# One TensorE kernel of two mixes and two grouped convolutions: the 32-column tiles of both convolutions put side by side

## The chip, the cores and the metric

The kernel runs on one core of one Trainium2 chip. The metric is the device time in microseconds of one execution; the time before is the median of three runs. The engines run beside each other and are kept in step by semaphores: TensorE (PE in the profile, its weight loads PEld), VectorE (DVE), ScalarE (ACT), GpSimd (POOL), and the queue of SyncE (SP) that issues the DMAs.

## The reference, cut to what matters

For each of 128 samples, x is 128 channels by 2048 points. Four layers are added to x one after the other; layers 0 and 2 are a mix of the channels with a matrix of the sample's own, layers 1 and 3 a grouped convolution with 9 taps.

```python
# layers 0 and 2
att = softmax(gelu(gelu(e @ W0 + b0) @ W1 + b1) @ W2 + b2)
agg_w = einsum('bk,koi->boi', att, weight[..., 0])
x = x + einsum('boi,bih->boh', agg_w, x) + (att @ bias_k)[:, :, None]
# layers 1 and 3
out = conv(x, weight, stride 1, padding 4, feature_group_count=4)   # 9 taps
x = x + out + einsum('nd,od->no', c, c_weight)[:, :, None] + side[None, :, None]
```

## The kernel before, in words

A sample's 2048 points are cut into 4 phases (point modulo 4) of 512 points, so a bank of PSUM (512 float32 a lane) holds one phase or one group. There are 4 groups of 32 channels, which are the four quarters of the lanes. The adding of x is an identity inside the weights.

A convolution is done for all 4 phases at once: of the 12 shifts (`SHIFTS`) between an input phase and an output phase, the 6 in the middle (`DENSE`) have weights for all four output phases and the 3 at either end only for one, two or three.

- `dense` (L348 to L364) does the 6 middle shifts. Each operand is split into a high and a low float32r part and three products are made (`PASSES`), for each of 4 groups: 6 x 3 x 4 = 72 matmuls with tiles of 32 rows by 128 columns. Four of them, one for each group, stand in the array side by side, so there are 18 rounds.
- `sparse` (L330 to L346) does the outer shifts with plain float32 operands. `NARROW` is one lot of tiles of 32 by 32, four output phases for each of four groups, 16 matmuls. `WIDE` is two lots of tiles of 32 by 64, two tiles for each of four groups, 8 matmuls each. The trace has two weight loads and two matmul records for each float32 matmul, so `NARROW` is 32 records of loads and each lot of `WIDE` 16.

A text here speaks of D for a stretch with 32x128 tiles, N for the 32x32 lot and W for the 32x64 lots, with the number of the layer: N1, W1, D1 for the first convolution (banks 4 to 7), N3, W3, D3 for the second (banks 0 to 3).

All engines run one program of steps `i` = 0 to 128, and the samples are pipelined over them. TensorE in step `i` (L390 to L413) does layer 1 of sample `i`, layer 3 of sample `i - 1`, layer 2 of sample `i` (`second_mix`, 48 matmuls of 32x128) and layer 0 of sample `i + 2` (`first_mix`, 12 matmuls of 128x128). Before the change its order is D1, N1, W1, W3, N3, D3, second mix, first mix. A matmul lot that ends a bank raises `mm[l]`.

What the other engines do in step `i`, in this order:

- ScalarE (L572 to L583): `full_0(i+1)` (bank to `y1_full`, frees banks 0 to 3), `high_2(i-1)`, `x_high(i+2)`, `high_1(i)` (waits for `mm[1]`, which the last lot of layer 1's `sparse` raises), `high_0(i+1)`, `output(i-1)` (waits for `mm[3]`, the end of D3), `full_2(i)` (waits for the second mix).
- VectorE: `matrix(0)` and `halves(0)` of sample i+2 (the last of it waits for the first mix before), `low_2(i-1)`, `x_low(i+2)`, `low_1(i)` (waits for `high_1`), `matrix(2)` and `halves(2)` of sample i+1, `low_0(i+1)`.
- GpSimd: small bias copies, and `in_time(i-2)` (L787), which waits until the shuffle DMAs have landed.
- SP (L226 to L239), strictly in order: the load of x, the store of the output, `store_matrix(i+1)` (waits for `own_set[2]`, the end of `halves(2)`), 16 shuffle DMAs of sample i-1, 4 loads of the mixing matrix (`load_matrix`, L207), which the next second mix needs.

D1 waits for `low_set[0]` (the end of `low_0`) and bank by bank for `full_2`; N3 or W3 reads `y3_full` and writes banks 0 to 3; D3 waits for `low_set[2]`; the second mix for `low_set[1]` and for its matrix.

Of the kernel before, what the change touches and what calls it, by code (L numbers as in the profile page):

```python
# [5 lines left out]
def build_cond_resid(nc, x, small, mix_w, mix_b, conv_w, consts, scratch, out):  # L6
# [10 lines left out]
    N = T // PH  # L17
# [7 lines left out]
    WIDE = (((1, 0, 2), (10, 2, 2)), ((2, 0, 2), (9, 2, 2)))  # L25
    NARROW = (((0, 0, 1), (9, 1, 1), (2, 2, 1), (11, 3, 1)),)
# [5 lines left out]
    with ctx:  # L32
        def sb(name, shape, dt=fp32):
            return ctx.enter_context(nc.sbuf_tensor(name, shape, dt))

        def sem(name):
            return ctx.enter_context(nc.semaphore(name))
# [4 lines left out]
        y1 = sb("y1", [128, 2, PH, HALO], f32r)  # L42
        y1_full = [sb(f"y1_full{b}", [128, PH, HALO]) for b in range(2)]
        y2 = sb("y2", [128, 2, G, N], f32r)
        y3 = sb("y3", [128, 2, PH, HALO], f32r)
        y3_full = sb("y3_full", [128, PH, HALO])
# [72 lines left out]
        conv_ident_set, conv_set = sem("conv_ident_set"), sem("conv_set")  # L119
# [18 lines left out]
        full_set = [sem(f"full_set{l}") for l in range(3)]  # L138
        high_set = [sem(f"high_set{l}") for l in range(3)]
        low_set = [sem(f"low_set{l}") for l in range(3)]  # L140
        phases_set = sem("phases_set")
# [16 lines left out]
        def has(i, inner, lag):  # L158

            return inner or 0 <= i - lag < B  # L160

        def nth(j, k):

            return 4 * j + k + 1
# [90 lines left out]
        def _(pe):  # L255
# [27 lines left out]
            for l in range(2):  # L283
                pe.wait_ge(att_set, l + 1)
                nc.tensor.matmul(ps[:, 2 + l, 0:K], ident[:, 0:1].broadcast_to([128, 128]), att_sb[:, l, :],
                                 start=True, stop=True).then_inc(att_first_mm, 1)
# [8 lines left out]
            def side_bias():  # L295

                pe.wait_ge(ctx_in, 16)
                pe.wait_ge(full_set[0], 2)
                for l in range(2):
                    for g in range(G):  # L300
                        last = nc.tensor.matmul(ps[:, l, g * B:(g + 1) * B], ctx_w_sb[:, l, g, :], emb_sb, start=True, stop=True)  # L301
                    last.then_inc(ctx_mm, 1)
# [24 lines left out]
                            if final:  # L327
                                ins.then_inc(mm[2], 1)

            def sparse(layer, src, begins, wait_bank):  # L330

                bank = 4 if layer == 1 else 0
                lots = WIDE + NARROW if begins else NARROW + WIDE
                for r, units in enumerate(lots):
                    for t in range(G):
                        rows = slice(CG * t, CG * (t + 1))
                        if r == 0 and begins:
                            wait_bank(t)
                        for s, p, width in units:
                            q, p_in = divmod(s, PH)  # L340
                            final = r == len(lots) - 1 and not begins
                            ins = nc.tensor.matmul(ps[CG * p:CG * (p + width), bank + t, :],  # L342
                                                   conv_raw[layer][rows, 128 * s + CG * p:128 * s + CG * (p + width)],
                                                   src[rows, p_in, q:q + N], start=(r == 0 and begins), stop=final)
                            if final:
                                ins.then_inc(mm[1], 1)  # L346

            def dense(layer, src, begins, wait_bank):  # L348

                bank = 4 if layer == 1 else 0  # L350
                order = sorted(DENSE, key=lambda s: (s % PH, s))
                for k, s in enumerate(order):
                    q, p_in = divmod(s, PH)
                    for n, (w, a) in enumerate(PASSES):
                        first = k == 0 and n == 0 and begins
                        final = k == len(order) - 1 and n == len(PASSES) - 1 and not begins
                        for t in range(G):
                            rows = slice(CG * t, CG * (t + 1))
                            if first:
                                wait_bank(t)  # L360
                            ins = nc.tensor.matmul(ps[:, bank + t, :], conv_parts[layer][rows, w, s - DENSE[0], :],  # L361
                                                   src[rows, a, p_in, q:q + N], start=first, stop=final)
                            if final:
                                ins.then_inc(mm[3], 1)  # L364

            def step(i, inner, odd):

                def free1(t):
                    if not inner and i == B - 1:
                        pe.wait_ge(full_set[2], 4 * i)  # L370
                    elif inner or i > 0:
                        pe.wait_ge(full_set[2], nth(i - 1, t))
                    elif t % 2 == 0:
                        pe.wait_ge(table_act, 2 - t // 2)
                    else:
                        pe.wait_ge(table_dve, 2 - t // 2)

                def free3(t):
                    if has(i, inner, -1):
                        pe.wait_ge(full_set[0], nth(i + 1, t))  # L380
                    else:
                        pe.wait_ge(phases_set, nth(i - 2, t))

                def free0(q):
                    if inner or i > 0:
                        pe.wait_ge(phases_set, nth(i - 1, q))
                    else:
                        pe.wait_ge(full_set[0], nth(1, q))

                if has(i, inner, 0):  # L390
                    if not inner and i == 0:
                        pe.wait_ge(zeros_set, 1)
                        pe.wait_ge(conv_set, 1)
                    pe.wait_ge(low_set[0], 4 * (i + 1))
                    dense(1, y1, True, free1)
                    if not inner and i == 0:
                        side_bias()
                        pe.wait_ge(full_set[0], G)
                    sparse(1, y1_full[odd], False, free1)
                if not inner and i == 0:  # L400
                    pe.wait_ge(ctx_read, 2)
                    first_mix(1, lambda q: pe.wait_ge(full_set[0], nth(0, q)))
                if has(i, inner, 1):
                    if not inner and i == 1:
                        pe.wait_ge(conv_set, 2)
                    pe.wait_ge(full_set[2], 4 * i)
                    sparse(3, y3_full, True, free3)
                    pe.wait_ge(low_set[2], 4 * i)
                    dense(3, y3, False, free3)
                if has(i, inner, 0):  # L410
                    second_mix(i)
                if has(i, inner, -2):
                    first_mix(i + 2, free0)  # L413
# [13 lines left out]
            for q in range(G):  # L427
                nc.tensor.matmul(ps[:, q, :], m_sum[0][:], x_t[:, q, :], start=True, stop=True).then_inc(mm[0], 1)  # L428
            att_to_all(1)
            all_steps(pe, step)  # L430
            last_regroup()

# [455 lines left out]
```

## Time and profile before

| | |
|---|---|
| median of 3 runs | 2650.08 us (2649.07 to 2650.8) |
| profiled execution, its own time | 2650.44 us |
| its span in the trace | 2648.6 us |
| PE busy | 2627.4 us (99%) |
| DVE busy | 2143.3 us (81%) |
| ACT busy | 2034.7 us (77%) |
| POOL busy | 818.0 us (31%) |
| L342 (`sparse`) matmuls | 16384 records, 753.8 us busy |
| L361 (`dense`) matmuls | 18432 records, 1141.7 us busy |

"Busy" is the time in which at least one instruction of the engine was under way. A matmul's end is modelled in the trace, so the start of the next weight load or matmul says more than a busy share. The difference between the profiled execution's own time and its span, 1.8 us, lies before the first and after the last instruction.

### The profile page before, as it was taken

The page shows a single profiled execution, that of the slowest core. Times are in us where ns is not written, and L with a number is a line of the kernel's source. Part 1 is how long each engine was busy: PE and PEld are TensorE (multiplying, and loading weights), DVE is VectorE, ACT ScalarE, POOL GpSimd, SP SyncE. Part 2 cuts the span into 40 slices and gives each one's busy share as a digit, 9 for nine tenths or more (in the row PEclk, how much of TensorE's full clock was granted, in tenths as well). Part 3 has the DMA queues.
Part 4 walks back from the last instruction along what each step waited for, and adds up shares of the span by engine and source line. Part 5 has one row for each costly group of instructions (what it writes and reads, how often), then busy time and mean ns, then how long its engine had stood idle before and what let it go on. Part 6 is the DMA issues. An engine that isn't in the chain of part 4 may idle for free.

```text
span 2648.6 us, 106673 instructions
## 1 busy us (share of the span) xinstructions
PE 2627.4 (99%) x42610; PEld 1808.4 (68%) x42610; DVE 2143.3 (81%) x3093; ACT 2034.7 (77%) x3605; POOL 818.0 (31%) x1040
## 2 busy tenths in 40 slices
PE   9999999999999999999999999999999999999997
PEld 6667666766676667666766676667666766676665
DVE  8888788878887888788878887888788878887884
ACT  7777777777777777777777777777777777777774
POOL 1233233323332333233323332333233323332332
PEclk9999999999999999999999999999999999999999
DMA  4565556555655565556555655565556555655554
GB/s 166 182 205 185 180 184 195 187 180 184 196 187 180 184 195 187 180 183 196 187 180 183 194 189 180 183 195 188 180 183 195 188 180 183 195 189 180 182 176 149
DMA packets 228046, 489.82 MB, mean 185 GB/s; under 512 B 47016, under 2 KB 129072, under 8 KB 195376
## 3 DMA queue, kind: packets, MB, share of 16 engines
q1 hardware_dynamic: 228016, 489.39, 58.7%
q8 instruction: 22, 0.36, 0.1%
q14 instruction: 8, 0.07, 0.0%
HBM read 205.04 MB, written 150.99 MB: 134 GB/s over the span
## 4 chain that ended last, share of the span: by engine, by line
PE 98%; DVE 1%; ACT 0%; issue 0%; DVEq 0%; ACTq 0%
PE ps L361 42%; PE ps L342 28%; PE ps L313 14%; PE ps L326 13%; DVE y L680 0%; DVE y L674 0%; DVE xp L652 0%; DVE m_sum L632 0%; DVE prod L627 0%; PE ps L259 0%; DVE y_full L703 0%; PE ps L428 0%; PE ps L301 0%; PE ps L264 0%; DVE x_t L715 0%
## 5 line engine op out<-in xcount | busy, mean ns | idle before, releaser
L361 PE MATMUL ps<-y,conv_parts 32*128 32x512 f32 x18432 | 1141.7, 395 | 3.9 <-DVE y_full L703 1.8
L361 PEld LDWEIGHTS ps<-y,conv_parts 32*128 32x128 f32 x18432 | 906.5, 183 | 283.1 <-issue 131.4
L781 POOL COPY bias<-bias_table 128x4 f32 (+3 forms) x512 | 317.6, 621 | 1795.5 <-DMA o_ch<-o_ph 896.9
L680 DVE TENSOR_TENSOR y<-y_full,y 128x512 fp32r<-128x512 f32 x1020 | 636.6, 688 | 221.9 <-ACT y L497 221.9
L342 PE MATMUL ps<-y_full,conv_raw 32*32 32x512 f32 (+1 forms) x16384 | 753.8, 596 | 1.7 <-DVE y_full L703 1.7
L491 ACT ACTIVATE y_full<-ps,bias 128x512 f32<-128x512 f32 x1016 | 602.6, 707 | 26.6 <-issue 16.2
L546 ACT ACTIVATE o_ph<-ps,bias 128x512 f32<-128x512 f32 x508 | 308.5, 693 | 371.5 <-PE ps L361 371.5
L497 ACT CAST y<-y_full 128x512 fp32r<-128x512 f32 x1020 | 566.8, 663 | 0.7 <-DVE y_full L703 0.7
L342 PEld LDWEIGHTS ps<-y_full,conv_raw 32*32 32x32 f32 (+1 forms) x16384 | 275.5, 116 | 408.4 <-issue 406.2
L787 POOL COPY o_t<-o_ch 128x512 f32<-128x512 f32 x508 | 528.5, 1186 | 26.9 <-DMA o_ch<-o_ph 26.9
L491 ACT ACTIVATE y<-ps,bias 128x512 fp32r<-128x512 f32 x516 | 313.0, 690 | 191.3 <-PE ps L342 176.6
L674 DVE SCALAR_TENSOR_TENSOR y<-ps,bias,y 128x512 fp32r<-128x512 f32 x516 | 352.0, 746 | 117.1 <-ACT y L491 117.0
L313 PE MATMUL ps<-xp,m_own 128*128 128x512 f32 x1524 | 386.9, 402 | 0.8 <-DVE xp L652 0.8
L326 PE MATMUL ps<-y,m_parts 32*128 32x512 f32 x6144 | 384.3, 391 | 0.8 <-DVE y L674 0.8
L627 DVE TENSOR_TENSOR prod<-mix_sb,att_table 128x1152 f32<-128x1152 f32 x254 | 379.3, 1493 | 0.0
L632 DVE TENSOR_REDUCE m_sum<-prod 128x128 f32<-128x1152 f32 x256 | 346.4, 1353 | 8.8
L326 PEld LDWEIGHTS ps<-y,m_parts 32*128 32x128 f32 x6144 | 335.8, 183 | 23.4 <-issue 1.6
L313 PEld LDWEIGHTS ps<-xp,m_own 128*128 128x128 f32 x1524 | 275.9, 187 | 105.5 <-issue 47.4
L652 DVE TENSOR_TENSOR xp<-x_t,xp 128x512 fp32r<-128x512 f32 x508 | 316.5, 686 | 0.0
L467 ACT CAST xp<-x_t 128x512 fp32r<-128x512 f32 x508 | 283.2, 671 | 0.6 <-DMA x_t<-x 0.6
L642 DVE CAST m_own<-m_sum 128x128 fp32r<-128x128 f32 x255 | 65.6, 257 | 119.7 <-PE ps L313 103.4
L645 DVE TENSOR_TENSOR m_own<-m_sum,m_own 128x128 fp32r<-128x128 f32 x255 | 74.6, 292 | 8.8
(60 smaller groups left out, 74.6 us busy)
## 6 DMA issues: line engine op xcount, KB each, us to landing
x_t<-x SPq DMA_DIRECT2D x128, 1024.0 KB, 5.0
o_ch<-o_ph SPq DMA_DIRECT2D x2032, 64.0 KB, 2.0
out<-o_t SPq DMA_DIRECT2D x127, 1024.0 KB, 4.0
m_parts<-mixed SPq DMA_DIRECT2D x512, 128.0 KB, 2.6
mixed<-m_own SPq DMA_DIRECT2D x128, 128.0 KB, 1.7
conv_raw<-conv_w SPq DMA_DIRECT2D x2, 768.0 KB, 9.8
mix_sb<-mix_w SPq DMA_DIRECT2D x2, 576.0 KB, 7.4
out<-x_t SPq DMA_DIRECT2D x4, 256.0 KB, 4.2
```

The costliest lines, as they stand in the source:

```text
L313: ins = nc.tensor.matmul(ps[:, q, :], m_own[0][:, m, :], xp[:, a, q, :], start=(n == 0), stop=(n == len(PASSES) - 1))
L326: ins = nc.tensor.matmul(ps[:, 4 + p, :], m_parts[rows, g, m, :], y2[rows, a, g, :], start=first, stop=final)
L342: ins = nc.tensor.matmul(ps[CG * p:CG * (p + width), bank + t, :], conv_raw[layer][rows, 128 * s + CG * p:128 * s + CG * (p + width)], src ...
L361: ins = nc.tensor.matmul(ps[:, bank + t, :], conv_parts[layer][rows, w, s - DENSE[0], :], src[rows, a, p_in, q:q + N], start=first, stop=f ...
L491: nc.scalar.activation(dst, src, ACT.Identity, bias=bias[layer][:, k % WIDTH[layer]:k % WIDTH[layer] + 1]).then_inc(done[layer], 1)
L497: nc.scalar.copy(dst, full).then_inc(high_set[layer], 1)
L627: nc.vector.tensor_tensor(prod[layer][:], mix_sb[layer][:], att.broadcast_to([128, C, K + 1]), ALU.mult).then_inc(scaled[layer], 1)
L632: nc.vector.tensor_reduce(m_sum[layer][:], prod[layer][:], AX_X, ALU.add).then_inc(summed[layer], 1)
L674: nc.vector.scalar_tensor_tensor(out=dst, in0=src, scalar=bias[layer][:, k % WIDTH[layer]:k % WIDTH[layer] + 1], in1=high.bitcast(fp32), o ...
L680: nc.vector.tensor_tensor(dst, full, high.bitcast(fp32), ALU.subtract).then_inc(low_set[layer], 1)
L781: nc.gpsimd.tensor_copy(bias[layer][:], bias_table[:, bass.ds(j, 1), COLUMN[layer]:COLUMN[layer] + WIDTH[layer]].rearrange("c j g -> c (j ...
L787: nc.gpsimd.tensor_copy(ov[:, p, :], o_ch[:, p, :]).then_inc(in_time_set, 1)
```

## The change

TensorE's order in a step becomes D1, N1, N3, W1, W3, D3, second mix, first mix: `sparse` is called with one list of lots at a time, N1 then N3, W1, W3. For i = 0 (no layer 3) and i = 128 (no layer 1) the missing ones are left out. The accumulation flags follow: N3 begins banks 0 to 3, the last lot of W1 ends banks 4 to 7 and raises `mm[1]`. The waits of layer 3 (`y3_full` whole, banks 0 to 3 free, and in step 1 the second convolution's low parts) move into `third_ready`, which `dense` calls for D1 before the last of its six shifts. Nothing is changed on other engines, and no matmul is added or taken away.

```diff
-            def sparse(layer, src, begins, wait_bank):
+            def sparse(layer, src, lots):
                 bank = 4 if layer == 1 else 0
-                lots = WIDE + NARROW if begins else NARROW + WIDE
                 for r, units in enumerate(lots):
...
-                            final = r == len(lots) - 1 and not begins
+                            final = layer == 1 and units is WIDE[-1]
...
-                                                   src[rows, p_in, q:q + N], start=(r == 0 and begins), stop=final)
+                                                   src[rows, p_in, q:q + N], start=(layer == 3 and units is NARROW[0]), stop=final)
...
+                    if k == len(order) - 1:
+                        wait_last()
...
-                def free3(t):
-                    if has(i, inner, -1):
-                        pe.wait_ge(full_set[0], nth(i + 1, t))
-                    else:
-                        pe.wait_ge(phases_set, nth(i - 2, t))
+                def third_ready():
+                    if not inner and i == 1:
+                        pe.wait_ge(conv_set, 2)
+                    if has(i, inner, 1):
+                        pe.wait_ge(full_set[2], 4 * i)
+                    if has(i, inner, 1) and has(i, inner, -1):
+                        pe.wait_ge(full_set[0], 4 * (i + 2))
+                    elif has(i, inner, 1):
+                        pe.wait_ge(phases_set, 4 * (i - 1))
...
-                    dense(1, y1, True, free1)
+                    dense(1, y1, free1, third_ready)
...
-                    sparse(1, y1_full[odd], False, free1)
+                    sparse(1, y1_full[odd], NARROW)
+                else:
+                    third_ready()
+                if has(i, inner, 1):
+                    sparse(3, y3_full, NARROW)
+                if has(i, inner, 0):
+                    sparse(1, y1_full[odd], WIDE)
...
-                    pe.wait_ge(full_set[2], 4 * i)
-                    sparse(3, y3_full, True, free3)
+                    sparse(3, y3_full, WIDE)
                     pe.wait_ge(low_set[2], 4 * i)
-                    dense(3, y3, False, free3)
+                    dense(3, y3, lambda t: None, lambda: None)
```

## Rows read from the trace of the kernel before

**Rows 1.** The page's chain that ended last, shares of the span by engine

```profile
PE 98%; DVE 1%; ACT 0%; issue 0%; DVEq 0%; ACTq 0%
```

**Rows 2.** Timeline, weight loads, one step: start us, length us, what, [idle before]

```profile
1000.29 4.04 PEld L361 LDWEIGHTS ps<-y,conv_parts 32*128 32x128 f32 x72 [0.36 <-issue]
1004.69 0.23 PEld L342 LDWEIGHTS ps<-y_full,conv_raw 32*32 32x32 f32 x32 [0.35 <-issue]
1005.76 0.29 PEld L342 LDWEIGHTS ps<-y_full,conv_raw 32*64 32x64 f32 x16 [0.84 <-issue]
1006.24 0.23 PEld L342 LDWEIGHTS ps<-y_full,conv_raw 32*64 32x64 f32 x8 [0.19 <-issue]
...
1008.39 0.23 PEld L342 LDWEIGHTS ps<-y_full,conv_raw 32*64 32x64 f32 x8 [0.20 <-issue]
1009.43 0.23 PEld L342 LDWEIGHTS ps<-y_full,conv_raw 32*32 32x32 f32 x32 [0.81 <-issue]
1010.51 4.02 PEld L361 LDWEIGHTS ps<-y,conv_parts 32*128 32x128 f32 x72 [0.84 <-issue]
...
1017.70 2.62 PEld L313 LDWEIGHTS ps<-xp,m_own 128*128 128x128 f32 x12 [0.37 <-issue]
1020.67 4.04 PEld L361 LDWEIGHTS ps<-y,conv_parts 32*128 32x128 f32 x72 [0.36 <-ACT y_full L491]
```

**Rows 3.** Timeline, ScalarE, the same step

```profile
1007.77 2.42 ACT L491 ACTIVATE y<-ps,bias 128x512 fp32r<-128x512 f32 x4 [1.47 <-PE ps L342]
...
1015.21 2.43 ACT L546 ACTIVATE o_ph<-ps,bias 128x512 f32<-128x512 f32 x4 [2.92 <-PE ps L361]
1017.86 4.74 ACT L491 ACTIVATE y_full<-ps,bias 128x512 f32<-128x512 f32 x8 [0.22 <-issue]
```

**Rows 4.** Timeline, VectorE, the same step and the head of the next

```profile
1008.49 2.73 DVE L674 SCALAR_TENSOR_TENSOR y<-ps,bias,y 128x512 fp32r<-128x512 f32 x4 [0.88 <-ACT y L491]
...
1014.53 0.29 DVE L645 TENSOR_TENSOR m_own<-m_sum,m_own 128x128 fp32r<-128x128 f32 x1
1014.74 2.49 DVE L680 TENSOR_TENSOR y<-y_full,y 128x512 fp32r<-128x512 f32 x4
...
1020.78 0.23 DVE L642 CAST m_own<-m_sum 128x128 fp32r<-128x128 f32 x1 [0.90 <-PE ps L313]
...
1023.13 2.50 DVE L680 TENSOR_TENSOR y<-y_full,y 128x512 fp32r<-128x512 f32 x4 [1.80 <-ACT y L497]
```

**Rows 5.** Timeline, SP's issues, the same step and the next

```profile
1015.92 10.04 SPq L214 DMA_DIRECT2D o_ch<-o_ph  x16
1026.15 1.88 SPq L207 DMA_DIRECT2D m_parts<-mixed  x4
```

**Rows 6.** Timeline, weight loads behind the last wait

```profile
2637.56 0.24 PEld L421 LDWEIGHTS ps<-y_full,consts_sb 32*32 32x32 f32 x32 [2.06 <-DVE y_full L710]
```

**Rows 7.** Timeline, weight loads of step 1

```profile
41.80 4.04 PEld L361 LDWEIGHTS ps<-y,conv_parts 32*128 32x128 f32 x72 [1.53 <-DVE y L680]
...
56.68 2.67 PEld L326 LDWEIGHTS ps<-y,m_parts 32*128 32x128 f32 x48 [0.66 <-issue]
```

**Rows 8.** Timeline, VectorE, step 1

```profile
44.91 0.95 DVE L602 TENSOR_TENSOR conv_parts<-conv_raw,conv_parts 128x768 fp32r<-128x768 f32 x1
...
53.84 2.72 DVE L674 SCALAR_TENSOR_TENSOR y<-ps,bias,y 128x512 fp32r<-128x512 f32 x4
```

**Rows 9.** Timeline, SP's issues, an early step (the fourth)

```profile
100.47 11.66 SPq L214 DMA_DIRECT2D o_ch<-o_ph  x16
112.40 3.21 SPq L207 DMA_DIRECT2D m_parts<-mixed  x4
```

**Rows 10.** Timeline, GpSimd, the same early steps

```profile
95.22 3.99 POOL L787 COPY o_t<-o_ch 128x512 f32<-128x512 f32 x4
...
115.60 3.98 POOL L787 COPY o_t<-o_ch 128x512 f32<-128x512 f32 x4
```

**Rows 11.** Timeline, VectorE, the same early step

```profile
96.75 2.58 DVE L642 CAST m_own<-m_sum 128x128 fp32r<-128x128 f32 x1
```

More of the change, by code:

```diff
@@ L336, in sparse, with dense @@
                         rows = slice(CG * t, CG * (t + 1))
-                        if r == 0 and begins:
-                            wait_bank(t)
                         for s, p, width in units:
                             q, p_in = divmod(s, PH)
-                            final = r == len(lots) - 1 and not begins
+                            final = layer == 1 and units is WIDE[-1]
                             ins = nc.tensor.matmul(ps[CG * p:CG * (p + width), bank + t, :],
                                                    conv_raw[layer][rows, 128 * s + CG * p:128 * s + CG * (p + width)],
-                                                   src[rows, p_in, q:q + N], start=(r == 0 and begins), stop=final)
+                                                   src[rows, p_in, q:q + N], start=(layer == 3 and units is NARROW[0]), stop=final)
                             if final:
                                 ins.then_inc(mm[1], 1)
-            def dense(layer, src, begins, wait_bank):
+            def dense(layer, src, wait_bank, wait_last):
+                begins = layer == 1
                 bank = 4 if layer == 1 else 0
@@ L403, in step @@
                 if has(i, inner, 1):
-                    if not inner and i == 1:
-                        pe.wait_ge(conv_set, 2)
-                    pe.wait_ge(full_set[2], 4 * i)
-                    sparse(3, y3_full, True, free3)
+                    sparse(3, y3_full, WIDE)
                     pe.wait_ge(low_set[2], 4 * i)
-                    dense(3, y3, False, free3)
+                    dense(3, y3, lambda t: None, lambda: None)
                 if has(i, inner, 0):
```

## The prediction, made before the changed kernel was run

> **What bounds the kernel now.** I read the chain that ended last first. It is TensorE for 98% of the span [rows 1], so a cut on any other engine is worth nothing, and a cut in TensorE's own time is worth its whole size as long as nothing else comes late. Next I read the timeline of the weight loads over one step, because a matmul's end is only modelled and a load's start is recorded [rows 2]. A step is 20.38 us (1000.29 to 1020.67). D1 runs to 1004.69, N1 to 1005.76, W1 with W3 to 1009.43, N3 to 1010.51, then D3, the second mix, the first mix from 1017.70. The reader is to look at the rhythm of the loads in the W stretch: after the first burst of 16, bursts of 8 start at 1006.24 and so on to 1008.39, six bursts, five intervals, 0.43 us each. Four lots of W follow each other there (two of layer 1, two of layer 3), each with two passes, and the step from layer 1 to layer 3, where the kernel has five waits, keeps the same rhythm. Each burst starts and ends inside the pass ahead of it. So, inside one tile shape, a pass costs 0.43 us and its loads nothing.
>
> Where the shape changes the rhythm breaks. N1 is two passes and should take 0.86 us; it takes 1.07 (1004.69 to 1005.76), and N3 1.08. The W stretch is eight passes, 3.44 us, and takes 3.67. Each visit to a shape thus pays 0.21 to 0.23 us beyond its passes: its first loads in the open and the emptying at the end.
>
> **The change part by part.**
>
> *Fewer visits.* Before, a step visits N, W, N between D1 and D3: 5.82 us. After, it visits N, W: N1 with N3 is four passes plus one visit's surcharge, 4 x 0.43 + 0.21 = 1.93 us, and W stays at 3.67, together 5.60. The cut is one surcharge, 0.21 (from N1), 0.22 (N3) or 0.23 (W); I take 0.215. The trace does not show two N lots in a row, nor W followed by D. For the first the nearest row is W to W, at no cost; for the second, N3 to D3 and N1 to W1 end after the same time (1.08 and 1.07) though the shape behind them differs, so I take leaving to cost the same whatever comes next. The bounds are 0.23 us a step as gain, and on the other side a gain of nothing, if the loads of N3 lay open as the first burst of a visit does (0.23 us for 32 of them). Below nothing lies only a shortage of instructions: the pair of N lots asks for 128 records in 1.93 us where the W rhythm asks for 16 in 0.43. If TensorE were fed no faster than the W rhythm, 37 records a microsecond, the second 64 would take 1.73 us in place of 0.86, a loss of up to 0.87 less 0.215 = 0.65 us a step. Against it stands the last regroup: after a wait of 2 us the 32 loads of 16 tiles of 32x32 start within 0.14 us (0.24 less one load of 0.10) [rows 6]. I take no shortage.
>
> *Number of steps.* Both convolutions meet in steps 1 to 127. Step 1 I count apart, the other 126 give 126 x 0.215 = 27.1 us. Steps 0 and 128 have the same visits before and after.
>
> *The waits of layer 3, earlier.* They come in D1 before the last sixth, about 3.4 us after D1's start (5/6 of 4.04). `full_0` is last there: it ends at 1017.86 + 4.74 = 1022.60, which is 1.93 us after D1's start [rows 3]. `full_2` ends before that. Slack 1.4 us. Queued behind the wait are the last 12 matmuls of D1 and N1, none of which would start otherwise either before 3.4 us. A wait that is already met costs nothing visible at the W1 to W3 seam [rows 2]; bounds zero to 0.05 us a step (the five at that seam stay inside a rhythm read to 0.01), taken at zero.
>
> *Layer 1's end, later.* `mm[1]` is now raised behind N3: two passes later, 0.86 us. In the old step `high_1` starts at 1007.77 and becomes 1008.6. It had waited 1.47 us, and ScalarE waits 2.92 us before `output` [rows 3]; of this 2.92 the delay and the earlier end of D3 (0.215) take 1.07 and leave 1.8. So `output`, `full_2` and `full_0` keep their places behind D3. On VectorE `low_1` ends at 1008.49 + 2.73 = 1011.22 and becomes 1012.1; the second mix begins when D3's loads end, 1014.53, now 1014.3: slack 2.2. `low_0` ends at 1017.23 and becomes 1018.1; the next D1 starts at 1020.67, now 1020.45: slack 2.4. `halves(0)` waited 0.90 us for the first mix [rows 4]; this wait goes (0.90 - 0.86 - 0.215), and VectorE is 0.2 us late there, which the 1.80 us ahead of `low_2` absorbs. What is late next is therefore still TensorE's own stream.
>
> *SP and GpSimd.* `halves(2)` ends at 1014.82 [rows 4], now 1015.7. The store behind it is ahead of the 16 shuffles in SP's order, so the shuffles start at most 0.86 us later (1.1 us lay between 1014.82 and their old start at 1015.92, part of it to spare). They last 10.04 us and the four matrix loads behind them end their issue at 1028.03, 6.9 us ahead of the second mix at 1034.9 (1014.53 + 20.38) [rows 2, 5]. With 0.86 us later there and a need 0.43 us earlier (two steps' cuts), 5.6 us are left, for loads that land a few us behind their issue. Hidden.
>
> *Step 1.* The second convolution's low parts end at 44.91 + 0.95 = 45.86 [rows 8]. They used to be needed at N3's side, now they are waited for before the last sixth of D1, at 41.80 + 3.4 = 45.2 [rows 7]. TensorE stands 0.7 us; against 0.215 saved this makes D3 end 0.5 us later. The second mix there waited for `low_1` (53.84 + 2.72 = 56.56, start 56.68), 0.26 us of it with TensorE empty. Loss 0.3 us.
>
> *Sum.* 27.1 - 0.3 = 26.8 us. From the profiled execution's 2650.44 us this gives 2623.6; that execution lies 0.36 above the median of the runs, so I forecast 2623.3.
>
> *A page's rule against it.* The W rows show loads starting in full overlap with matmuls of the same four row groups [rows 2]. The Trainium skill, "TensorE: Matmul & The Clock Gate", Part 3, section "The mechanism", says that a weight load overlaps matmuls under way only when its row group is another one. By that rule N3's loads would wait for N1 in each row group, and its 0.23 us of loads would eat the saving: a sum of 2650. The trace's W rows disagree with it.
>
> **The rivals.**
>
> *The second N lot pays for its loads after all* (the mechanism of that sentence, kept for 16 tiles at once). For it: no row shows 16 tiles reloaded while they run; N has twice W's loads per pass. Against: W's burst of 8 takes 0.23 of 0.43 us and N's 32 take the same 0.23, so 16 have room. Price: 0.23 back of 0.215, no change, 2650; if half of them lie open 0.1 back, 2636.
>
> *The ring of SP and GpSimd becomes the bound.* In an early step shuffles, matrix loads, landing and `in_time` form a ring: `in_time` starts at 95.22 and at 115.60, 20.38 us apart, with the shuffles at 11.66 us instead of 10.04 and the matrix loads issued until 115.61 [rows 9, 10], and VectorE's cast takes 2.58 us beside `in_time`, where an undisturbed one takes 0.23 [rows 4, 11]. `in_time`'s end frees the output store, the cast's end the matrix store, and both are ahead of the shuffles on SP. If that ring stays at 20.38 or more while TensorE would like 20.16, it never recovers, the matrix comes late, and the gain is lost; with VectorE's 0.2 us of lateness inside it the step would be up to 20.38 + 0.2. That is 2650 to 2675 (126 x 0.2 = 25); its middle, 2663, stands for this rival. It decides from a ring of 20.38 us on. Against: in the old steady step the shuffles wait for `output` and not for the ring, with a cast of 0.23 us, and `in_time` has fallen back by itself.
>
> *Starved instructions*: up to 0.65 us a step as worked out, 2730 at the most; by [rows 6] unlikely.
>
> *A smaller surcharge saved*: if two joined N lots still cost 0.05 us at the seam, the gain is 126 x 0.165 = 21, 2629.
>
> **How the numbers follow.** Forecast as worked out, 2618 to 2627: 0.76. Smaller surcharge or half-open loads, 2627 to 2640: 0.14. Loads fully open, near 2650: 0.04. Ring: 0.04. Starved: 0.02. The range is 2617 to 2632; its lower end is 0.26 us saved a step, a bit over the W surcharge, its upper end 0.14. About 0.2%, 5.3 us, is what a measurement here can tell from no change. Faster by more: 0.90; within: 0.05; slower: 0.05.
>
> **What would show it.** Right: step length 20.16 us; 64 loads of 32x32 with one break of rhythm, N1 with N3 lasting 1.93 us; W at 3.67; `high_1`'s wait longer, `output`'s wait about 1.8 us, `halves(0)`'s wait gone. Wrong: a gap of 0.2 us between the two N bursts; matmuls of N3 spread out; weight loads of D1 or the second mix with a releaser on VectorE, ScalarE or DMA; casts of over 1 us in the middle of the run.

## The result and the profile after

The changed kernel takes 2659.22 us (median of 7 runs, 2658.56 to 2660.43) against 2650.8 us for the kernel before in 7 runs of the same sessions. The ratio is 1.0032, with a 95% interval of 1.0023 to 1.0042: slower by 8.4 us, beyond what the runs scatter. The forecast was 2623.3 with a range of 2617 to 2632. The sign was wrong, and the measured time lies 27 us above the range.

The page after shows the same picture as a whole. First its span and engine line, then its chain by engine, which answers to [rows 1]:

```profile
span 2656.6 us, 106246 instructions
PE 2635.7 (99%) x42610; PEld 1777.5 (67%) x42610; DVE 2103.8 (79%) x3093; ACT 2034.0 (77%) x3605; POOL 751.5 (28%) x1040
...
PE 98%; DVE 1%; issue 0%; ACT 0%; DVEq 0%; ACTq 0%
```

TensorE is still 98% of the chain, and its granted clock was 0.998 to 0.999 here and in every other run of this document, so the time has to be looked for inside its own stream. The timeline of the weight loads over one step, the view of [rows 2]:

```profile
1003.22 4.04 PEld L361 LDWEIGHTS ps<-y,conv_parts 32*128 32x128 f32 x72 [0.36 <-issue]
1007.62 0.23 PEld L339 LDWEIGHTS ps<-y_full,conv_raw 32*32 32x32 f32 x32 [0.35 <-issue]
1008.07 0.10 PEld L339 LDWEIGHTS ps<-y_full,conv_raw 32*32 32x32 f32 x1 [0.22 <-issue]
1008.50 0.55 PEld L339 LDWEIGHTS ps<-y_full,conv_raw 32*32 32x32 f32 x31 [0.32 <-issue]
1009.89 0.23 PEld L339 LDWEIGHTS ps<-y_full,conv_raw 32*64 32x64 f32 x16 [0.84 <-issue]
1010.38 0.18 PEld L339 LDWEIGHTS ps<-y_full,conv_raw 32*64 32x64 f32 x8 [0.25 <-issue]
...
1013.51 4.02 PEld L361 LDWEIGHTS ps<-y,conv_parts 32*128 32x128 f32 x72 [0.81 <-issue]
...
1020.70 2.62 PEld L313 LDWEIGHTS ps<-xp,m_own 128*128 128x128 f32 x12 [0.37 <-issue]
1023.68 4.04 PEld L361 LDWEIGHTS ps<-y,conv_parts 32*128 32x128 f32 x72 [0.36 <-ACT y_full L498]
```

A table of the two steps, each length the difference of two starts in these rows and in [rows 2]:

| stretch | before, us | after, us |
|---|---|---|
| D1 | 4.40 | 4.40 |
| N1 and N3 | 1.07 + 1.08 | 2.27 |
| W1 and W3 | 3.67 | 3.62 |
| D3 and second mix | 7.19 | 7.19 |
| first mix | 2.97 | 2.98 |
| step | 20.38 | 20.46 |

Steps of 20.46 and 20.43 alternate in the changed kernel, 0.065 us a step more than before on the mean, and 126 x 0.065 = 8.2 us is nearly the whole difference (8.4 measured, 8.0 between the spans). The change lies in two rows; the alternation lies in D3 and the second mix (7.19 and 7.17). W is 0.05 shorter. The pair of N lots, forecast at 1.93, takes 2.27, and that is more than the two lots took apart.

The third and fourth rows show how. N1's 32 loads come at once at 1007.62. At 1008.07, when N1's second pass starts, exactly one load of N3 is there; the next is at 1008.50, when that tile's first pass starts, and it is the same tile's second load. Then nothing. The instructions of that line in the gap from 1008.52 to 1008.69 and in the 0.4 us around it:

```profile
L339 PEld LDWEIGHTS ps<-y_full,conv_raw x1: 105/105/105, 1008.5 to 1008.5; 32*32 32x32 f32 x1
...
L339 PEld LDWEIGHTS ps<-y_full,conv_raw x13: 101/102/105, 1008.5 to 1008.8; 32*32 32x32 f32 x13
```

From the records of the single instructions (their starts in ns): N1's first second-pass matmul starts at 1008072 and a pass takes 427 to 429 ns, so it has streamed through at about 1008500. (This is what "complete" means below, the start of the last pass plus one pass. The end that the trace models for this matmul, 1008072 + 587 = 1008659, lies 0.16 us later.) The second tile of N3 loads at 1008690, and the 14 tiles behind it follow 16 to 17 ns apart, the last at 1008923. In N1, the tiles came 6 to 7 ns apart. So 15 of 16 tiles of N3 come late: 0.19 us after the first matmul of N1 is complete, and then at the pace of 17 ns a matmul. That is 0.19 + 14 x 0.0167 less the 0.10 that the lot's own spread takes anyway = 0.32 us, nearly the whole difference of 0.34 between 2.27 and 1.93.

The other engines' rows moved the way that was forecast. ScalarE and VectorE, answering to [rows 3] and [rows 4]:

```profile
1011.90 2.42 ACT L498 ACTIVATE y<-ps,bias 128x512 fp32r<-128x512 f32 x4 [2.69 <-PE ps L339]
...
1018.22 2.43 ACT L553 ACTIVATE o_ph<-ps,bias 128x512 f32<-128x512 f32 x4 [1.80 <-PE ps L361]
1020.86 4.74 ACT L498 ACTIVATE y_full<-ps,bias 128x512 f32<-128x512 f32 x8 [0.22 <-issue]
```

```profile
1018.60 2.49 DVE L687 TENSOR_TENSOR y<-y_full,y 128x512 fp32r<-128x512 f32 x4
...
1023.88 0.23 DVE L649 CAST m_own<-m_sum 128x128 fp32r<-128x128 f32 x1
...
1026.14 2.50 DVE L687 TENSOR_TENSOR y<-y_full,y 128x512 fp32r<-128x512 f32 x4 [1.71 <-ACT y L504]
```

`output` waits 1.80 us for D3, as forecast; `halves(0)` waits no longer; `low_0` ends at 1021.09, 2.6 us ahead of the next D1. None of them holds TensorE. The 1.80 is a hit by two errors that cancel: `high_1` starts 8.68 us behind D1's start and not 7.48, which is 1.20 later where 0.86 was forecast, and D3 starts 0.07 later where 0.215 earlier was forecast.

### The profile page after: what moved, and what is told of

Same layout as the page of the kernel before. It is cut to its first block, busy times and chain, and to the rows that moved or that the text cites. A ratio compares the mean times of both kernels' runs of the same rounds, so it can differ in the third digit from the quotient of the medians.

```text
span 2656.6 us, 106246 instructions
## 1 busy us (share of the span) xinstructions
PE 2635.7 (99%) x42610; PEld 1777.5 (67%) x42610; DVE 2103.8 (79%) x3093; ACT 2034.0 (77%) x3605; POOL 751.5 (28%) x1040
## 4 chain that ended last, share of the span: by engine, by line
PE 98%; DVE 1%; issue 0%; ACT 0%; DVEq 0%; ACTq 0%
PE ps L361 42%; PE ps L339 28%; PE ps L313 14%; PE ps L326 13%; DVE y L681 0%; DVE y L687 0%; DVE m_sum L639 0%; PE ps L259 0%; DVE prod L634 0%; DVE y_full L710 0%; ACT y L504 0%; DVE xp L659 0%; ACT y L498 0%; PE ps L435 0%; PE ps L301 0%
## 5 line engine op out<-in xcount | busy, mean ns | idle before, releaser
L339 PE MATMUL ps<-y_full,conv_raw 32*64 32x512 f32 (+1 forms) x16384 | 764.0, 596 | 1.6 <-DVE y_full L710 1.6
L788 POOL COPY bias<-bias_table 128x4 f32 (+3 forms) x512 | 235.5, 460 | 1869.3 <-DMA o_ch<-o_ph 944.3
L339 PEld LDWEIGHTS ps<-y_full,conv_raw 32*64 32x64 f32 (+1 forms) x16384 | 269.5, 117 | 428.0 <-issue 415.3
L794 POOL COPY o_t<-o_ch 128x512 f32<-128x512 f32 x508 | 522.5, 1156 | 27.0 <-DMA o_ch<-o_ph 27.0
L326 PEld LDWEIGHTS ps<-y,m_parts 32*128 32x128 f32 x6144 | 318.5, 183 | 40.1 <-issue 1.0
L634 DVE TENSOR_TENSOR prod<-mix_sb,att_table 128x1152 f32<-128x1152 f32 x254 | 345.0, 1358 | 0.0
```

Of the source, the lines that this page charges most:

```text
L326: ins = nc.tensor.matmul(ps[:, 4 + p, :], m_parts[rows, g, m, :], y2[rows, a, g, :], start=first, stop=final)
L634: nc.vector.tensor_tensor(prod[layer][:], mix_sb[layer][:], att.broadcast_to([128, C, K + 1]), ALU.mult).then_inc(scaled[layer], 1)
L794: nc.gpsimd.tensor_copy(ov[:, p, :], o_ch[:, p, :]).then_inc(in_time_set, 1)
```

## The experiments

The theory that I formed on these rows: **TensorE takes only 64 records of loads and matmuls into its queue, and a place comes free when the matmul is complete.** A float32 matmul is four records, so 16 fit. A lot of W is 8 matmuls: the lot that runs and the next one fit together, and the rhythm never breaks. A lot of N is 16 and fills the queue alone; one more matmul is at the door, the rest enter only as N1's are completed. The Trainium skill, "TensorE: Matmul & The Clock Gate", gives 64 as TensorE's queue depth in the table at its head; the trace agrees in the counts (16 matmuls of four records, and the numbers below).

Its rivals: that a 32x32 tile which is busy can't be reloaded under way (the rule of the Trainium skill, "TensorE: Matmul & The Clock Gate", Part 3, section "The mechanism", that the prediction set aside); that the loss belongs to how the pair is entered; that another engine pays for layer 1's later end; and that a change of tile shape had never cost what [rows 2] seemed to say.

### Lots of 8 and of 12

In these three runs, the 32-column tiles of two or of one of the four channel groups are left out of the computation, so that a lot is smaller. The edit, in `sparse` (T = 2 or 3), with the beginning flag moved to `WIDE` for the groups left out:

```diff
                     for t in range(G):
+                        if t >= T and units is NARROW[0]:
+                            continue
                         rows = slice(CG * t, CG * (t + 1))
```

Lots of 8, order of the changed kernel:

> Left out of the computation: the 32-column tiles of two of the four channel groups, so a lot of them is 8 matmuls and not 16. Order of the changed kernel (both lots side by side). Full-queue theory (TensorE holds 16 float32 matmuls until they complete; in the changed kernel the first lot fills it, one tile of the second lot loads early and the other 15 start to enter 0.19 us after the first matmul of the first lot is done): 8 + 8 fit, so all 8 loads of the second lot come at the first lot's second pass, its matmuls start without a gap, and both lots last 4 x 0.43 + about 0.2 = 1.9 us in place of 2.27; the step is 0.15 to 0.25 us shorter than with the old order and the same lots. Reload theory (a busy 32x32 tile can't be reloaded under way, as the page's rule on row groups has it): one load early and then a gap of 0.19 us as in the changed kernel, 2.15 us or more for both lots, the step no shorter than with the old order. Lateness theory (another engine pays for the later end of layer 1): the seam is as it is in the changed kernel and the step is made longer elsewhere.

Lots of 8, order of the kernel before:

> Left out: the same half of the 32-column tiles. Order of the kernel before. This is what the other run with 8-tile lots is compared with. All theories: each lot still takes two passes, 1.0 to 1.07 us, and the step stays at 20.3 to 20.38 us. Full-queue theory adds that the 64-column lots behind the first small lot start with loads 7 ns apart and not 17, since a lot of 8 leaves the queue room for them.

Lots of 12, order of the changed kernel:

> Left out: the 32-column tiles of one of the four channel groups, so a lot is 12 matmuls. Order of the changed kernel. Full-queue theory: 12 + 4 fit and one more is at the door, so 5 tiles of the second lot load at the first lot's second pass, the other 7 not until 0.19 us after the first matmul is done; both lots last about 2.2 us. Reload theory: one tile early, as with 16.

The first took 2608.33 us and the second 2629.34 (one run each, the kernel before beside them 2649.43). With lots of 8 the change is a gain: 21.0 us. Timeline of the weight loads with lots of 8 side by side:

```profile
1009.18 0.18 PEld L341 LDWEIGHTS ps<-y_full,conv_raw 32*32 32x32 f32 x16 [0.35 <-issue]
1009.63 0.15 PEld L341 LDWEIGHTS ps<-y_full,conv_raw 32*32 32x32 f32 x8 [0.28 <-issue]
1010.06 0.15 PEld L341 LDWEIGHTS ps<-y_full,conv_raw 32*32 32x32 f32 x8 [0.28 <-issue]
1011.05 0.23 PEld L341 LDWEIGHTS ps<-y_full,conv_raw 32*64 32x64 f32 x16 [0.84 <-issue]
```

The loads of the second lot come in full, eight at each pass, and the pair takes 1.87 us, 4 x 0.43 + 0.15. The mean step is 20.03 us against 20.21 with the same lots in the old order (20.18 and 20.24 by turns), 0.18 less: near the forecast's 0.215. A tile of 32x32 under way can be reloaded like any other. The reload theory falls, and so does lateness: layer 1 ends late by its second lot here too, and the gain stays.

The third took 2643.55 us. Its loads:

```profile
1001.52 0.21 PEld L341 LDWEIGHTS ps<-y_full,conv_raw 32*32 32x32 f32 x24 [0.35 <-issue]
1001.98 0.13 PEld L341 LDWEIGHTS ps<-y_full,conv_raw 32*32 32x32 f32 x5 [0.25 <-issue]
1002.41 0.42 PEld L341 LDWEIGHTS ps<-y_full,conv_raw 32*32 32x32 f32 x19 [0.30 <-issue]
1003.66 0.23 PEld L341 LDWEIGHTS ps<-y_full,conv_raw 32*64 32x64 f32 x16 [0.84 <-issue]
```

Five early loads, no more and no fewer: 16 places less 12, and the one at the door. 8 early with lots of 8, 5 with 12, 1 with 16 is the count that a queue of 16 such matmuls gives. The pair takes 2.14 us (2.2 expected).

The old order with lots of 8, for the seam into W, which was a side forecast:

```profile
1017.24 0.18 PEld L344 LDWEIGHTS ps<-y_full,conv_raw 32*32 32x32 f32 x16 [0.35 <-issue]
1018.26 0.23 PEld L344 LDWEIGHTS ps<-y_full,conv_raw 32*64 32x64 f32 x16 [0.84 <-issue]
...
1021.88 0.18 PEld L344 LDWEIGHTS ps<-y_full,conv_raw 32*32 32x32 f32 x16 [0.81 <-issue]
```

W's first 16 loads take 0.23 us here and W 3.62, where behind a lot of 16 they took 0.29 and 3.67 [rows 2]. That is the 0.05 us by which W is shorter in the changed kernel: there too it starts on a full queue, that is, its matmuls already stand in the queue when its turn comes. The step, forecast at 20.3 to 20.38, came out at 20.21 instead, since each lot takes 1.02 and not 1.07, and W 3.62.

### Counted in records or in matmuls, and a fixed time or a share of a pass

In this one the 32-column tiles are bfloat16 views of the same words, each lot given twice:

```diff
-                for r, units in enumerate(lots):
+                for again, units in enumerate([u for u in lots for _ in range(2 if lots is NARROW else 1)]):
...
+                            if width == 1:
+                                raw = conv_raw[layer][:].bitcast(mybir.dt.bfloat16)
+                                act_in = src[:].bitcast(mybir.dt.bfloat16)
+                                c0 = 2 * (128 * s + CG * p)
+                                nc.tensor.matmul(ps[CG * p:CG * (p + 1), bank + t, :], raw[rows, c0 + 1:c0 + 2 * CG:2],
+                                                 act_in[rows, p_in, 2 * q + 1:2 * (q + N):2], start=(layer == 3 and again == 0), stop=False)
+                                continue
```

> Changed in the computation: the 32-column tiles take the upper halves of the float32 words as bfloat16, one load and one matmul record each in place of two of each, and each lot is given twice, so that there are four lots of 16 matmuls, one pass of 0.21 us each. Order of the changed kernel. Full queue counted in records (64): 32 such matmuls fit, the loads of the second lot come while the first runs, there is no gap of 0.19 us at that seam, and the four lots last 1.1 to 1.4 us. Full queue counted in matmuls (16): a gap of 0.2 to 0.35 us at each of the three seams, 1.7 to 2.1 us.

It took 2516.67 us. The loads of the four lots, the second row cut to the first 0.33 us:

```profile
1014.18 0.91 PEld L343 LDWEIGHTS ps<-y_full,conv_raw 32*32 32x32 bf16 x64 [0.35 <-issue]
...
1014.18 0.34 PEld L343 LDWEIGHTS ps<-y_full,conv_raw 32*32 32x32 bf16 x33 [0.35 <-issue]
...
1015.33 0.23 PEld L346 LDWEIGHTS ps<-y_full,conv_raw 32*64 32x64 f32 x16 [0.24 <-issue]
```

33 loads come before the first lot's first place is free, 32 and one at the door, where in float32 it is 17 matmuls. In the records of the single instructions the 34th load comes at 1014610, 0.19 us after the first matmul's pass ends (1014423), so the gap is there again, one lot later. Four passes of 0.21 take 1.15 us, in the range for records (1.1 to 1.4) and far from that for matmuls (1.7 to 2.1). So the queue doesn't count matmuls. It counts 64 records of loads and matmuls, or 32 pairs of a load and its matmul; every load here has its own matmul, and no run tells these two apart.

In the other one the 32-column tiles work on 256 of their 512 points, and those of layer 3 are overwritten:

```diff
-                            ins = nc.tensor.matmul(ps[CG * p:CG * (p + width), bank + t, :],
+                            n = N // 2 if width == 1 else N
+                            ins = nc.tensor.matmul(ps[CG * p:CG * (p + width), bank + t, 0:n],
...
-                                                   src[rows, p_in, q:q + N], start=(layer == 3 and units is NARROW[0]), stop=final)
+                                                   src[rows, p_in, q:q + n], start=(layer == 3 and units is not WIDE[1]), stop=final or (layer == 3 and width == 1))
```

> Left out: the 32-column tiles compute 256 of their 512 points (and those of layer 3 are overwritten), so one of their passes is 0.21 us and not 0.43. Order of the changed kernel. Full-queue theory: what is lost at the seam is a fixed time (0.19 us from the completion of the first matmul, then 17 ns for each tile), so both lots last about 0.88 + 0.21 + 0.21 + 0.1 = 1.4 us and not 4 x 0.21 + 0.21 = 1.06. Theory that the loss is a share of a pass (a missed slot): (2.27 - 0.21) / 2 + 0.21 = 1.24 us. No loss: 1.06.

It took 2567.39 us. Its pair:

```profile
1013.74 1.16 PEld L340 LDWEIGHTS ps<-y_full,conv_raw 32*32 32x32 f32 x64 [0.35 <-issue]
1015.31 0.23 PEld L340 LDWEIGHTS ps<-y_full,conv_raw 32*64 32x64 f32 x16 [0.41 <-issue]
```

1.57 us, where no loss is 1.06, a share of a pass 1.24 and a fixed time was worked out at 1.4. The records of the single instructions show the same 0.19 us between the completion of N1's first matmul (its second pass starts at 1013980 and takes 216 ns, to 1014196) and the next tile's load (1014386), and the same 17 ns after it. What 1.4 left out is one more wait: the last tile of N3 loads at 1014764, 161 ns behind its neighbour at 1014603 where the others stand 17 apart. So the 0.19 us and the 17 ns are fixed times, not shares of a pass. The loss as a whole is larger here (1.57 less 1.06, 0.51 us) than with whole passes (0.34); 0.14 to 0.16 of that is the last tile's wait, and why it waited again was not settled.

### Whether the way into the pair matters, and what a change of shape costs

W first and the pair last (128, 64, 32, 32, 128), the semaphore of layer 1 raised by eight of the 16 matmuls of its N lot (`final and p % 2`):

```diff
-                    sparse(1, y1_full[odd], NARROW)
+                    sparse(1, y1_full[odd], WIDE)
...
-                    sparse(3, y3_full, NARROW)
+                    sparse(3, y3_full, WIDE)
...
-                    sparse(1, y1_full[odd], WIDE)
+                    sparse(1, y1_full[odd], NARROW)
...
-                    sparse(3, y3_full, WIDE)
+                    sparse(3, y3_full, NARROW)
```

> Nothing left out. Order of a step: 128-column tiles, the four 64-column lots, then both 32-column lots, 128-column tiles. Full-queue theory: the same gap between the two 32-column lots (one load early, 15 of them 0.19 us after the first matmul is done), whatever stands ahead of them; the 64-column stretch starts with a full queue, loads 7 ns apart, and lasts 3.62 us and not 3.67; step 20.40 to 20.45. Theory that the gap comes from the way the pair is entered (from 128-column tiles): it goes here, pair 1.93 us, step 20.1.

It took 2680.22 us, more than expected, with a step of 20.61. The loads:

```profile
1015.23 0.23 PEld L339 LDWEIGHTS ps<-y_full,conv_raw 32*64 32x64 f32 x16 [0.35 <-issue]
...
1018.85 0.29 PEld L339 LDWEIGHTS ps<-y_full,conv_raw 32*32 32x32 f32 x32 [0.81 <-issue]
1019.31 0.10 PEld L339 LDWEIGHTS ps<-y_full,conv_raw 32*32 32x32 f32 x1 [0.17 <-issue]
1019.74 0.73 PEld L339 LDWEIGHTS ps<-y_full,conv_raw 32*32 32x32 f32 x31 [0.32 <-issue]
1021.31 1.71 PEld L361 LDWEIGHTS ps<-y,conv_parts 32*128 32x128 f32 x32 [0.84 <-issue]
```

One early load again, then the gap; W in 3.62. The entrance doesn't matter for the gap. But the pair takes 2.46 and not 2.27: the last 31 loads spread over 0.73 us and not 0.55.

The order with the same lots never side by side (128, 32, 64, 32, 64, 128), made by moving the call for N3 behind W1:

```diff
-                if has(i, inner, 1):
-                    sparse(3, y3_full, NARROW)
                 if has(i, inner, 0):
                     sparse(1, y1_full[odd], WIDE)
...
                 if has(i, inner, 1):
+                    sparse(3, y3_full, NARROW)
                     sparse(3, y3_full, WIDE)
```

> Nothing left out. Order of a step: 128-column tiles, 32, 64 (layer 1), 32, 64 (layer 3), 128-column tiles: five visits' borders in place of four, and no lot of 16 directly behind another of its shape. If a change of tile shape costs what the prediction took (about 0.215 us: the wait until all has ended, and the first loads in the open), the step is 20.38 + 0.2 = 20.6 us and the kernel some 27 us slower than before. If the surcharge per visit was only the queue's refill and a change of shape is free by itself, the step stays near 20.4.

It took 2698.24 us, with a step of 20.76, 0.38 more than before and not 0.2. The loads of N1, W1, N3, W3 and the D3 behind them:

```profile
1001.75 0.23 PEld L339 LDWEIGHTS ps<-y_full,conv_raw 32*32 32x32 f32 x32 [0.35 <-issue]
1002.83 0.29 PEld L339 LDWEIGHTS ps<-y_full,conv_raw 32*64 32x64 f32 x16 [0.84 <-issue]
...
1004.78 0.41 PEld L339 LDWEIGHTS ps<-y_full,conv_raw 32*32 32x32 f32 x32 [0.81 <-issue]
1006.04 0.23 PEld L339 LDWEIGHTS ps<-y_full,conv_raw 32*64 32x64 f32 x16 [0.84 <-issue]
...
1007.94 4.03 PEld L361 LDWEIGHTS ps<-y,conv_parts 32*128 32x128 f32 x72 [0.81 <-issue]
```

Each W visit of four passes (1.71 us) takes 1.95 and 1.90: a visit's surcharge is 0.24 and 0.19, as the prediction had it, and it isn't only the queue. The two visits take 3.85 where one took 3.67, 0.18 more; about as much, 0.18, is in N3, 1.26 where it was 1.08. Its 32 loads spread over 0.41 us. Both surprises have one feature in common: the matmuls whose places the late tiles wait for raise a semaphore. In the records the late entries come 42 ns apart behind a matmul that raises one and 17 ns behind one that doesn't; in the run with W first they alternate (1020.26, 1020.28, 1020.32, 1020.34).

### Half of the semaphore increments

Both runs again with four increments by 2 in place of eight by 1:

```diff
-                            if final:
-                                ins.then_inc(mm[1], 1)
+                            if final and p:
+                                ins.then_inc(mm[1], 2)
```

(in the one with W first, `final and p == 3` in place of `final and p % 2`).

> Nothing left out. The run with the order 128, 32, 64, 32, 64, 128 again, but the last lot of layer 1's 64-column tiles raises its semaphore on four matmuls (by 2 each) and not on all eight (by 1 each). In that run the matmuls that enter the full queue behind matmuls with an increment came 42 ns apart, those behind matmuls without one 17 ns. Theory that the increment itself holds the place in the queue some 26 ns longer: the last seven loads of the second 32-column lot come 42 and 17 ns apart by turns, that lot is about 0.09 us shorter (1.26 to 1.17) and the step 20.67 in place of 20.76. Theory that the lot is slow for another reason (a change of shape right behind a stretch of only four passes): nothing moves.

> Nothing left out. The run with both 32-column lots behind the 64-column lots again, layer 1's 32-column lot now with four increments (by 2) and not eight (by 1). Increment theory: in the second 32-column lot only every fourth gap between entries is 42 ns, the pair is 0.1 us shorter (2.46 to 2.36), the step 20.51 in place of 20.61. The 0.19 us from the first completion to the second tile's load stay. Otherwise: nothing moves.

The first took 2685.86 us (2698.24 with eight), the second 2672.31 (2680.22). N3 of the first and the pair of the second:

```profile
1020.40 0.32 PEld L339 LDWEIGHTS ps<-y_full,conv_raw 32*32 32x32 f32 x32 [0.81 <-issue]
1021.56 0.23 PEld L339 LDWEIGHTS ps<-y_full,conv_raw 32*64 32x64 f32 x16 [0.84 <-issue]
```

```profile
1016.25 0.29 PEld L339 LDWEIGHTS ps<-y_full,conv_raw 32*32 32x32 f32 x32 [0.81 <-issue]
...
1017.14 0.63 PEld L339 LDWEIGHTS ps<-y_full,conv_raw 32*32 32x32 f32 x31 [0.32 <-issue]
1018.61 4.03 PEld L361 LDWEIGHTS ps<-y,conv_parts 32*128 32x128 f32 x72 [0.84 <-issue]
```

The load bursts shrink from 0.41 to 0.32 and from 0.73 to 0.63, N3 from 1.26 to 1.16 and the pair from 2.46 to 2.36, as expected. The steps go from 20.76 to 20.67 as expected, and from 20.61 to 20.55 where 20.51 was expected: the pair lost its 0.10, while D3 with the second mix and the first mix together took 0.04 more. (The steps say more than the times of the kernels here: the kernel before took 2647.63 beside these two runs, and 2649.43 and 2650.83 beside the ones with eight, so against the kernel before beside them they are 10.6 and 4.7 us better.) An increment on a matmul holds its place some 26 ns longer. (The Trainium skill, "TensorE: Matmul & The Clock Gate", section "The cost: per-tile semaphore tail", has 26.3 ns for an increment; the 25 to 26 ns between the two spacings agree.) In the changed kernel itself no increment is in the way: N3 waits for N1, which raises nothing.

### A way round that didn't pay

If a lot of 16 must not follow another and W likes a full queue, N1 can go ahead of D1. Its wait for the last bank's copy then has to stand on the last matmul of the first mix:

```diff
+                    early = inner or 0 < i <= B - 2
+                    if early:
+                        sparse(1, y1_full[odd], True, lambda t: None, NARROW)
                     pe.wait_ge(low_set[0], 4 * (i + 1))
-                    dense(1, y1, True, free1)
+                    dense(1, y1, not early, free1)
...
-                    first_mix(i + 2, free0)
+                    first_mix(i + 2, free0, lambda: pe.wait_ge(full_set[2], 4 * (i + 1)))
```

> Nothing left out. The kernel before, but in steps 1 to 126 layer 1's 32-column lot stands ahead of its 128-column tiles (32, 128, 64, 32, 128); as many changes of shape as before. No lot of 16 follows another, and the 64-column stretch is entered from a full queue, not from one that a 32-column lot has just emptied: its loads start 7 ns apart and not 17, and it lasts 3.62 in place of 3.67 us. Full-queue theory: the step is 0.05 us shorter than before, 126 x 0.055 = 7 us, 2644. Shape-change-only theory: as before, 2651. If the wait for the last bank's copy, moved to the last matmul of the first mix, comes late: 0.1 us a step, 2660.

It took 2662.01 us in 5 runs (2661.62 to 2663.27), against 2650.83 for the kernel before in 9 runs: ratio 1.0042, interval 1.0029 to 1.0056. The loads of two steps' heads:

```profile
1003.55 0.19 PEld L315 LDWEIGHTS ps<-xp,m_own 128*128 128x128 f32 x1 [0.19 <-ACT y_full L496]
1003.98 0.23 PEld L344 LDWEIGHTS ps<-y_full,conv_raw 32*32 32x32 f32 x32 [0.24 <-issue]
1005.05 4.05 PEld L363 LDWEIGHTS ps<-y,conv_parts 32*128 32x128 f32 x72 [0.84 <-issue]
1009.46 0.23 PEld L344 LDWEIGHTS ps<-y_full,conv_raw 32*64 32x64 f32 x16 [0.35 <-issue]
...
1013.08 0.29 PEld L344 LDWEIGHTS ps<-y_full,conv_raw 32*32 32x32 f32 x32 [0.81 <-issue]
...
1024.41 0.39 PEld L344 LDWEIGHTS ps<-y_full,conv_raw 32*32 32x32 f32 x32 [0.24 <-issue]
1025.64 4.05 PEld L363 LDWEIGHTS ps<-y,conv_parts 32*128 32x128 f32 x72 [0.84 <-issue]
```

W is 3.62 as wanted. The wait for `full_2` comes late by 0.19 us at the end of the first mix, and in the second of these steps 0.23 us late; there N1's own loads spread over 0.39 us and N1 takes 1.23 in place of 1.07. So it goes by turns over the whole run: 1.07 in one step, 1.13 to 1.23 in the next. The third case of its expectation (2660) came true in number, but the late wait itself is the smaller part. Over these two steps the first mix takes 0.04 and 0.07 us longer than before, N1 nothing and 0.16, N3 0.05 in both (1.13), and W 0.05 less. No order that I tried beats the kernel before.

## Why the prediction was wrong

- **What bounds the kernel**: right. TensorE is 98% of the chain after as before, and the difference is found in its stream to 0.2 us.
- **The surcharge of a visit, 0.21 to 0.23 us**: right in size. A visit more costs 0.19 to 0.24 (order alternated); with lots of 8, which leave the queue room, the change brings 0.18 us a step. With 16 it was there too, but something larger came with it.
- **"The nearest row is W to W, at no cost"**: this is the step that failed. It took the rhythm inside a shape as a property of the shape. It was one of the lot's size: two W lots are 16 float32 matmuls and just fit TensorE's queue, two N lots are 32 and don't. The term was 4 x 0.43 + 0.21 = 1.93 and measured 2.27. The 0.34 us too little outweighs the saving.
- **"I take no shortage"**: wrong, with the working next to it that would have said otherwise. The shortage was listed with a bound of 0.65 us a step and a chance of 0.02, on the strength of [rows 6]. That row shows 32 loads within 0.14 us behind a wait, but they are the loads of exactly 16 matmuls, which by the count above could all stand in the queue already; a queue that is full at the start says nothing of how it is filled. What fills it can be read at the seam N1 to W in [rows 2]: 16 loads over 0.29 us instead of 0.23, which I didn't ask about.
- **W stays at 3.67**: 3.62. Small, in the kernel's favour, from the same cause: W now starts on a full queue.
- **The rule of the Trainium skill on row groups** ("TensorE: Matmul & The Clock Gate", Part 3, section "The mechanism"): setting it aside was right (lots of 8 reload under way). The queue depth of 64 in the table at the head of that page of the Trainium skill was the figure to weigh; the trace has four records to a float32 matmul.
- **Waits of layer 3 ahead of D1's last sixth**: nothing a step, as taken (D1 4.40 before and after). In step 1 TensorE stood 0.75 us for the low parts, 0.7 forecast, and the step took 21.08 us where it had taken 20.89:

```profile
45.58 0.53 PEld L361 LDWEIGHTS ps<-y,conv_parts 32*128 32x128 f32 x12 [0.75 <-DVE conv_parts L609]
```

- **Later end of layer 1**: hidden, as worked out, though `high_1` came 1.20 us later and not 0.86: `output`'s wait is 1.80 (1.8 forecast, by two errors that cancel), `halves(0)`'s is gone.
- **Ring of SP and GpSimd**: did not decide. The steady step has GpSimd's `in_time` and the undisturbed cast of 0.23 us in their old order, and TensorE waits for neither. In one early step of either kernel the second mix waits for its matrix's DMA (0.29 us after, 0.33 before). The measured 2659 lies inside this rival's 2650 to 2675, and that is chance: its mechanism is not in the trace.

The balance per step, from the terms as measured: W -0.05, the two N lots from 2.15 to 2.27, +0.12; +0.07 (0.065 on the mean of the two alternating steps), and 126 of them 8.2 us.

## What to carry to other kernels

A rhythm read between two lots holds only for lots of that many matmuls: before putting lots side by side, count the records of loads and matmuls that the running lot and the next one hold together (here 64 fit, four to a float32 matmul, two to a bfloat16 one) and look at a seam where a lot fills the queue. Splitting work over more, smaller tiles that run at once makes lots that fill the queue alone; a change of shape between two such lots can be the cheaper neighbour, as here (1.07 + 1.08 us apart, 2.27 side by side). That the refill then hides in the emptying that the change costs anyway is my reading of it, not tested. Where a burst of loads is longer at one seam than at another of the same shape (0.29 and 0.23 us), its last matmuls did not yet stand in the queue when its turn came.

## What the runs showed of the hardware that I had not expected

- When TensorE's queue is full, the next load starts 0.19 us after a matmul's last pass has streamed through (1008500 to 1008690 ns; 1014196 to 1014386 with half columns). That is 0.03 us after the end that the trace models for that matmul (1008659; 1014354), so the 0.19 may be for the most part the matmul's own end. From then on float32 matmuls enter 17 ns apart, against 6 to 7 ns when they stand ready.
- One matmul beyond those that fit starts its load early: 17 float32 matmuls, 33 bfloat16 ones.
- A semaphore increment on a matmul delays the entry behind it from 17 to 42 ns. Halving eight of them to four gave 0.09 and 0.06 us a step; in the kernels' times, against the kernel before beside each, 10.6 and 4.7 us (one run each).
- Behind a wait that came 0.19 us late the 32 loads of a lot of 16 took 0.23 us, behind one that came 0.23 us late 0.39. Why so small a difference costs 0.16 us was not settled.
